# Softmax row sums in a conditioned attention kernel: VectorE adds one pair of slabs per half head, GpSimd chains two more adds to it, TensorE sums two slabs a head instead of four

## The reference

```python
h = _sln(hidden, w, ln_g, ln_b, Wg, bg, Wb, bb)          # conditioned layer norm
qkv = (h @ Wqkv.T + bqkv).reshape(B, N, num_heads, hd, 3)
energy = jnp.einsum('bhqd,bhkd->bhqk', q, k)
att = jax.nn.softmax(energy, axis=-1) / D ** 0.5
out = jnp.einsum('bhqk,bhkd->bhqd', att, v)
out = out @ Wp.T + bp                                     # heads side by side again
h1 = out + hidden
h2 = _sln(h1, w, ln_g, ln_b, Wg, bg, Wb, bb)
return h2 + h1
```

## Time and profile before

| | us |
|---|---|
| median of 3 runs | 1395.69 (1395.29 to 1397.49) |
| profiled execution | 1395.35 |
| its span, first to last instruction | 1393.7 |
| PE busy | 1331.2 (96%) |
| POOL busy | 984.6 (71%) |
| DVE busy | 909.3 (65%) |
| ACT busy | 701.5 (50%) |

### The profile page before, as it was taken

The page is one execution under the profiler, slowest core; times in us unless marked ns, Lnnn a source line. Parts: engine busy times, 40 slices in busy tenths (PEclk is TensorE's granted clock), DMA queues, the critical chain, the costliest instruction groups (busy, mean ns, idle before and its releaser), DMA issues.

```text
span 1393.7 us, 34891 instructions
## 1 busy us (share of the span) xinstructions
PE 1331.2 (96%) x10948; PEld 928.2 (67%) x10948; DVE 909.3 (65%) x1634; ACT 701.5 (50%) x1374; POOL 984.6 (71%) x755
## 2 busy tenths in 40 slices
PE   6898999999999999999999999999999999999993
PEld 4897676767676767777676767677656555655562
DVE  5345767667676767676776767666666667666535
ACT  4221455555555555555555555555564646565341
POOL 1443175656666688979787888877797969797845
PEclk8899899999999999999999999999999999999997
DMA  7577534443443545645453544626463424253321
GB/s 245 155 209 221 131 93 108 111 106 116 106 115 86 151 107 144 154 124 147 113 159 88 165 118 140 155 77 165 103 168 85 116 80 119 83 137 92 87 56 64
DMA packets 216709, 174.17 MB, mean 125 GB/s; under 512 B 105492, under 2 KB 186516, under 8 KB 216632
## 3 DMA queue, kind: packets, MB, share of 16 engines
q1 hardware_dynamic: 214456, 166.83, 44.7%
q0 software_dynamic: 1984, 6.29, 1.2%
q10 hardware_dynamic: 192, 0.07, 0.0%
HBM read 113.29 MB, written 58.51 MB: 123 GB/s over the span
## 4 chain that ended last, share of the span: by engine, by line
PE 83%; DVE 5%; SPq 4%; issue 3%; DMA 2%; ACT 1%; POOL 1%; DVEq 1%; POOLq 0%; ACTq 0%
PE ps_o L851 15%; PE ps_st L834 15%; PE ps_a L820 12%; PE ps_w L725 10%; PE ps_w L783 9%; PE ps_s L864 8%; PE ps_st L820 4%; PE ps_st L783 3%; DVE half_max L1360 3%; PE ps_w L898 1%; PE ps_w L771 1%; PE ps_s L876 1%; PE ps_s L783 1%; PE ps_o L725 1%; ACT p L1129 1%
## 5 line engine op out<-in xcount | busy, mean ns | idle before, releaser
L1129 ACT ACTIVATE p<-ps_st 128x512 f32<-128x512 f32 x864 | 484.7, 600 | 436.9 <-PE ps_st L834 433.1
L1360 DVE TENSOR_REDUCE half_max<-ps_a 128x1 f32<-128x512 f32 x729 | 484.6, 685 | 256.4 <-PE ps_a L820 254.1
L1642 POOL TENSOR_TENSOR p<-p 128x1024 f32<-128x1024 f32 x208 | 493.4, 2392 | 220.2 <-PE ps_o L851 219.3
L834 PE MATMUL ps_st<-q_stack,k_stack 98*128 98x512 f32 x1024 | 415.7, 408 | 8.4 <-DMA q_stack<-max_rows 4.6
L820 PE MATMUL ps_a<-k_stack,q_stack 96*128 96x512 f32 x729 | 305.8, 421 | 12.7 <-DVE half_max L1360 10.0
L834 PEld LDWEIGHTS ps_st<-q_stack,k_stack 98*128 98x128 f32 x1024 | 195.1, 191 | 72.9 <-ACT p L1129 38.0
L851 PE MATMUL ps_o<-p,v_head 128*32 128x256 f32 x3456 | 209.2, 382 | 0.0
L1360 DVE TENSOR_REDUCE half_max<-ps_st 128x1 f32<-128x512 f32 x231 | 158.3, 685 | 70.7 <-PE ps_st L820 70.7
L820 PEld LDWEIGHTS ps_a<-k_stack,q_stack 96*128 96x128 f32 x729 | 138.0, 190 | 88.0 <-issue 40.8
L783 PEld LDWEIGHTS ps_w<-hT_s,wqkv_s 128*128 128x128 f32 x1056 | 157.2, 190 | 20.1
L851 PEld LDWEIGHTS ps_o<-p,v_head 128*32 128x32 f32 x3456 | 110.1, 110 | 78.4 <-issue 5.0
(11 more groups left out here) (199 smaller groups left out, 1361.7 us busy)
## 6 DMA issues: line engine op xcount, KB each, us to landing
qk_scratch<-qkT_s SPq DMA_DIRECT2D x108, 256.0 KB, 2.4
q_stack<-qk_scratch SPq DMA_DIRECT2D x192, 128.0 KB, 2.6
k_stack<-qk_scratch SPq DMA_DIRECT2D x192, 128.0 KB, 2.8
x_tile<-in_x SPq DMA_DIRECT2D x34, 256.0 KB, 4.9
gq_s<-gain_bias_scratch SPq DMA_DIRECT2D x16, 512.0 KB, 4.3
v_scratch<-v_parts SPq DMA_DIRECT2D x32, 256.0 KB, 3.3
v_head<-v_scratch SPq DMA_DIRECT2D x64, 128.0 KB, 2.1
att_scratch<-o_stage SPq DMA_DIRECT2D x240, 32.0 KB, 1.5
```

The source lines that it names most:

```text
L834: pe.matmul(ps_st[:, (ST_BANK_WIDE if wide else ST_BANK)[2 * k + e], :], k_stack[0:98, s, k * 128:(k + 1) * 128], q_stack[0:98, s, e * 512 ...
L1129: nc.scalar.activation(p_of(step // 8, tiles)[:, k, e * 512:(e + 1) * 512], ps_st[:, (ST_BANK_WIDE if tiles else ST_BANK)[2 * k + e], :], ...
L1360: V.tensor_reduce(half_max[:, s % 2, item:item + 1], A_BANK[bank], AX.X, ALU.max).then_inc(a_used, 1)
L1642: G.tensor_tensor(p[:, slot, :], p[:, slot - 2, :], p[:, slot, :], ALU.add).then_inc(pair_added, 1)
```

## The change

- **DVE** gets a new instruction per half head, `slab_add`: it adds slab 0 of the half to slab 1 (128 x 1024, both inputs and the output in SBUF), once `pv_done` says that these two are weighted. It stands in step k = 4 (first half) and in step k = 0 of the next head (second half), behind the ring items and the projection result of that step.
- **POOL** still does two adds per half, now in a chain: slab 2 onto slab 3 when all four are weighted, then slab 1 (which holds 0 + 1) onto slab 3, which waits for DVE's add and for its own first add.
- **PE** sums slots 3 and 7 only (`chain_sum`), one slab per burst, and in iterations 0 to 10 the burst too has the four weighted slabs first and the sum behind them.
- **ACT**'s waits for free slots follow: slot k % 4 = 0 waits for `slab_added`, 1 and 2 for `pair_added`, 3 for `sum_done`.
- Iteration 11 is written out on its own for DVE, as it already is for the others.

```diff
-        SUM_SLOT = [2, 3, 6, 7]
+        SUM_SLOT = [3, 7]
...
-            def pair_sums(g, s, j, near=False):
+            def chain_sum(g, s, h, near=False):
...
-                pe.wait_ge(pair_added, 16 * g + 4 * s + j + 1)
+                pe.wait_ge(pair_added, 16 * g + 4 * s + 2 * h + 2)
                 for e in range(4):
-                    mm = pe.matmul(ps_s[HD * e:HD * e + HD, 0:QW], root_s[:], p_of(s, near)[:, SUM_SLOT[j], e * QW:(e + 1) * QW],
-                                   start=(j == 0), stop=(j == 3))
+                    mm = pe.matmul(ps_s[HD * e:HD * e + HD, 0:QW], root_s[:], p_of(s, near)[:, SUM_SLOT[h], e * QW:(e + 1) * QW],
+                                   start=(h == 0), stop=(h == 1))
...
                         if k == 0 and behind and (not last or finishing):
-                            if mode == "bare":
+                            if not last:
                                 for j in range(4, 8):
                                     weighted(*before, j, near=near)
-                            for j in (0, 1):
-                                pair_sums(*before, j, near=near)
-                            if mode != "bare":
+                            chain_sum(*before, 0, near=near)
+                            if last:
...
+                freed, count = {0: (slab_added, 2 * v + half + 1), 1: (pair_added, 4 * v + 2 * half + 2),
+                                2: (pair_added, 4 * v + 2 * half + 1), 3: (sum_done, 2 * v + half + 1)}[k % 4 if paired else 3]
...
+            def slab_add(g, s, h, near):
+
+                dve.wait_ge(pv_done, 16 * g + 4 * s + 2 * h + 1)
+                p = p_of(s, near)
+                V.tensor_tensor(p[:, 4 * h + 1, :], p[:, 4 * h, :], p[:, 4 * h + 1, :], ALU.add).then_inc(slab_added, 1)
...
                         if tiles and fill in range(2, 8):
                             take(i + LEAD, fill)
+                        if k == 0 and not (first and s == 0) and not (last and s > 0):
+                            slab_add(i - (s == 0), (s - 1) % 4, 1, tiles or (joining and s == 0))
+                        if k == 4 and not last:
+                            slab_add(i, s, 0, tiles)
...
             def pair_add(g, s, j, near=False):
 
-                slot = SUM_SLOT[j]
-                pool.wait_ge(pv_done, 16 * g + 4 * s + 2 * (j // 2) + 2)
+                h, total = j // 2, 16 * g + 4 * s
                 p = p_of(s, near)
-                G.tensor_tensor(p[:, slot, :], p[:, slot - 2, :], p[:, slot, :], ALU.add).then_inc(pair_added, 1)
+                if j % 2:
+                    pool.wait_ge(slab_added, 8 * g + 2 * s + h + 1)
+                    pool.wait_ge(pair_added, total + j)
+                else:
+                    pool.wait_ge(pv_done, total + 2 * h + 2)
+                G.tensor_tensor(p[:, 4 * h + 3, :], p[:, 4 * h + 2 - j % 2, :], p[:, 4 * h + 3, :], ALU.add).then_inc(pair_added, 1)
```

More of the change, by code:

```diff
@@ L218, in conditioned_attention @@
         pv_done = sem("pv_done")
+        slab_added = sem("slab_added")
         pair_added = sem("pair_added")
@@ L1002, in iteration @@
                         if k == 4 and behind and (not last or finishing):
[L1003 to L1007 removed]
+                            chain_sum(*before, 1, near=near)
                         if k % 2 and last:
@@ L1126, in exps @@
                     if e == 0:
-                        need(act, pair_added if paired and k not in SUM_SLOT else sum_done, freed)
+                        need(act, freed, count)
                     nc.scalar.activation(p_of(step // 8, tiles)[:, k, e * 512:(e + 1) * 512], ps_st[:, (ST_BANK_WIDE if tiles else ST_BANK)[2 * k + e], :], ACT.Exp
```

24 lines of the change are left out of this document (10 added, 14 removed).

## The result

| | before | changed |
|---|---|---|
| median, us | 1395.99 (4 runs, 1395.29 to 1397.49) | 1416.32 (4 runs, 1415.06 to 1420.34) |
| ratio, 95% interval | | 1.0149 (1.0127 to 1.0171) |
| span of the profiled execution | 1393.7 | 1413.4 |
| iterations 0 to 10 | | +6.8 |
| iterations 11 to 14 | | +10.9 |

What follows compares the result with a forecast made beforehand. PE, 96% busy, was taken as the bound, with DVE and POOL possibly making it wait. Span 1393.7 - 51.6 + 27.3 + 3.5 + 20.0 = 1392.9 us; forecast 1395 us, no change, range 1358 to 1425.

Steps and rivals of the forecast that it cites:

- PE's gain: Heads 0 to 59: PE sums one slab less per half, 120 x 0.43 = -51.6 us.
- lost starts and POOL, iterations 0 to 10: DVE's add waits behind POOL's 26 times, +27.3 us; POOL's lost time in iterations 4 to 10, +3.5 us.
- iterations 11 to 14, gain and cost together: DVE's adds delay POOL's gapless chain and PE's sums, +20.0 us, set against PE's saving there.
- second rival: DVE and POOL do not exclude each other to speak of; only PE's saving counts: 1344 us (1340 to 1350), 10%.
- first rival: DVE starts first everywhere in iterations 0 to 10, so the 27.3 fall away: 1368 us (1358 to 1382), 20%.
- the price of a lost start: POOL's add holds DVE's, and PE's fourth item behind the burst waits 1.0 to 1.1 us, taken as 1.05.
- a ring that lets PE run three items ahead: Step 4's burst: an undisturbed DVE add ends 0.6 us late, which this room was to make free for PE.
- In step 12 POOL is then in a short instruction: Iterations 4 to 10: POOL's 1.3 us instruction lets DVE go early enough, so only steps 4 and 8 lose.
- 0.5 per iteration: Iterations 4 to 10: POOL's lost time reaching ACT and the output's steps, 7 x 0.5 = +3.5 us.
- The sum at 1185.58 comes 3.6 late: Iterations 11 to 14: four DVE adds (steps 8 to 20) move the end of POOL's adds from 1184.79 to 1189.2.
- full gain of 3.4 an iteration: Iterations 11 to 14: PE's saving if nothing held it, 8 x 0.43 us.
- third rival: Iterations 0 to 10: lag is handed on, 44 of 87 bursts lost instead of 26: 1415 us (1403 to 1440), 30%.

Runs made afterwards that it cites:

- first experiment: Changed kernel with DVE's add replaced by a TENSOR_REDUCE of one slab (one SBUF input), slab 0 left out of the row sums: 1361.38 us, 0.9749.
- third experiment: Changed kernel with one wait moved, so POOL's first add of a half waits for DVE's add too: 1382.95 us, 0.9902.
- fifth experiment: Changed kernel with the ring's one two-bank place in iterations 0 to 10 moved from step 10 to step 25: 1411.5 us, 1.0102.

## Why the prediction was wrong, step by step

| term | forecast | measured |
|---|---|---|
| PE's gain, iterations 0 to 10 (88 slabs) | -37.8 | -36.0 (first experiment) |
| lost starts and POOL, iterations 0 to 10 | +30.8 | +42.8 (6.8 + 36.0) |
| iterations 11 to 14, gain and cost together | +6.2 (20.0 - 13.8) | +10.9 |
| start and iteration 15 | 0 | +2.0 |
| span against 1393.7 | -0.8 | +19.7 |

Of the 20.5 us between the two, 12.0 are the lost starts, 4.7 iterations 11 to 14, 1.8 PE's gain, and 2.0 the start and the last iteration, which vary as much from one execution to another.

**Right.** The burst takes 2.30 us (2.29 said) and each slab is worth 0.42. The two engines exclude each other for whole instructions: 1.21 us for DVE's add when free (1.25 said), 3.05 to 3.75 behind POOL's (about 3.4 said). POOL starts at 2.05 (2.3 to 2.4 behind a transfer), and DVE loses steps 4, 8 and 12 of iterations 1 to 3, the margin at step 12 being 0.05. The order of the burst costs nothing. The handing on from step 4 to step 8 is shown by the kernel without the wait at step 8. The second rival (no exclusion, 1344) falls with the first experiment: taking the exclusion away moves 55 us. The first rival's condition, DVE first everywhere in iterations 0 to 10, is what the third experiment made: 1383 and not 1368, for iterations 5 to 9 gain 2.0 instead of 3.4 each and 11 to 14 cost 14. Its 1368 is near the 1367.5 of the kernel that forces DVE first and has the old sums in 11 to 14, but its terms are others: -29.0 and +3.1 for the two stretches, where the rival had -34.3 and +6.2.

**The step that failed is the price of a lost start, "1.0 to 1.1 us, take 1.05", used for every step.** It measured 1.7 us on average, 42.9 us for 25 losses. The number of losses was right by luck, 25 against 26 (see *Which iterations*). Per loss, as the difference of the changed kernel and the first experiment's, from burst to burst:

| step | losses | each | sum |
|---|---|---|---|
| 4 | iterations 1 to 3 and 5 to 9 | 1.2 (1 to 3), 1.5 (5 to 9) | 11.4 |
| 8 | the same eight | 2.0 (iterations 2, 3, 5, 6), 3.5 (1, 7, 8, 9) | 22.0 |
| 12 | the same eight | 1.05 | 8.4 |
| 28 | iteration 10 | 1.1 | 1.1 |

- *Step 8* costs 13.6 more than eight times 1.05. The prediction took its ring room ("a ring that lets PE run three items ahead") from step 4, but the table of banks has its one place with two banks just behind the burst of step 8: one item less ahead, 0.95 more (fifth experiment). In four of eight cases the granted clock then falls to its lower level for some 3.4 us, 1.5 more.
- *Step 4* in 5 to 9 costs 1.5, since POOL issues a transfer first (L1569) and starts its add at 2.3 to 2.4, not 2.05, and DVE loses to it all the same.
- *Which iterations.* Iterations 0 and 4 lost nothing (DVE comes at 2.02 in steps 4 and 12 there and at 1.87 in step 8), 5 to 9 lost step 12 on top, and iteration 10 lost step 28 in place of 4 and 8. "In step 12 POOL is then in a short instruction" was true of the trace of before but not after two lost starts, which gave POOL 3.5 us of time. Seven too many (iterations 0, 4, 10) and six too few cancel but for one. And the "0.5 per iteration" for POOL didn't show: the same delays covered it. Where they are taken away, it is 1.4 per iteration in 5 to 9.
- *Iterations 11 to 14: the place of the late sum was wrong.* The prediction had it in step 24 ("The sum at 1185.58 comes 3.6 late"). In the changed kernel the sum of that step doesn't wait; PE waits 1.45 in step 12 and 3.48 in step 16. The size is near, by luck. The tighter place stands in the trace of before, POOL and PE in step 16 of iteration 13:

```profile
1165.73 4.73 POOL L1642 TENSOR_TENSOR p_far<-p_far 128x1024 f32<-128x1024 f32 x2
...
1170.39 1.05 PE L864 MATMUL ps_s<-p_far,root_s 128*32 128x256 f32 x16
```

POOL's second add ends at 1170.46, and PE's first sum starts at 1170.39: it needed the first add only. The one sum of the changed kernel needs both, so each 0.43 us that PE comes sooner is a wait. In step 24 the room was 0.79. Undersized was the clock: 12.6 us from the burst of step 16 to the next, where before it took 7.4. More basic: the full gain of 3.4 an iteration was never there. With no DVE work at all PE still waits in step 16, and iterations 13 and 14 come to -0.3 and +1.3. POOL's chain is the bound, as the 230 of 270 busy us and "end just ahead of their sum" in the prediction say; the sum still credited PE's saving.
- *Iterations 11 and 12* are not like 13 and 14, though the part ahead of the prediction takes the iterations of a stretch as alike. In their step 20 PE waits for a transfer, 1.26 us in iteration 11 before, and in 12:

```profile
1113.08 0.79 PE L834 MATMUL ps_st<-q_stack,k_stack 98*128 98x512 f32 x1 [2.59 <-DMA q_stack<-max_rows]
```

The clock was at its lower level as that wait ended and behind it. In the kernels with the old sums the wait is 1.0 to 3.0 us; where PE is late at the sum of step 16 already, in the changed kernel, it is under 0.6. So the four iterations together vary from 0.0 to +3.1 between kernels that are alike there, and the 2.6 gained without DVE work come from iteration 12, where that kernel waits 1.1 for the transfer. Iterations 13 and 14 are steady: together +0.1 to +0.4 in those kernels, +1.0 without DVE work, +9.2 in the changed one.
- *The third rival* had the sign and, by luck, the time (its own sum gives 1414), but not the mechanism: the lag was handed on as it says, but 25 starts were lost and not 44; the cost was in the price of each.

**What stays open**: why the clock fell behind four of eight equal waits; why DVE loses to a POOL instruction that comes straight behind the issue of a transfer, though its own recorded start, within that issue, is 0.10 to 0.37 us ahead; and whether it is the add's second input or its wide output that shuts POOL out.

## What to carry to other kernels

A new DVE instruction with two SBUF inputs beside a busy POOL should be costed by who starts first, and the order should be fixed by a wait, not left to a margin of 0.05 us: turning it round was worth 33 us here, about as much as the best kernel here gained over the kernel before. Price a stall at each place it can fall, with the room that the buffers have *there* and the clock behind it, and not by the first place looked at. And before an engine's saving is credited in a stretch, ask who comes second there: where POOL ends just ahead of PE's sum, less work on PE buys nothing.
